# Two more split units a round, as halves through a PSUM bank, in a recommendation tower on one core

## What is computed

```python
for i, (W, b) in enumerate(zip(Ws, bs)):          # three layers, 128 maps each
    z = einsum('bfd,bgd->bfgd', x, h)             # x: (1024, 39, 16), h: 39, then 64 maps
    cur = relu(einsum('bfgd,fgl->bld', z, W) + b)
    if i != 2: h, direct = cur[:, :64], cur[:, 64:]
    else:      direct = cur
    outs.append(direct)
z = concat(outs).sum(-1)                          # over d
h = relu(concat([z, dense_ctx]) @ W_top1 + b_top1)
h = relu(h @ W_top2 + b_top2)
y = h @ W_top3
```

## Time and profile before

| | |
|---|---|
| median of 3 runs | 1290.84 us (1286.87 to 1290.93) |
| the profiled execution's own time | 1292.15 us |
| its span | 1290.1 us |
| granted TensorE clock, mean | 0.996 |
| busy: TensorE, VectorE, ScalarE, GpSimd | 96%, 81%, 58%, 83% |

### The profile page before, as it was taken

One profiled execution on the slowest core, in us unless ns is written; L12 is line 12 of the kernel. 1 busy time (PEld: TensorE's weight loads), 2 busy tenths in 40 slices (PEclk: granted clock), 3 DMA queues, 4 the chain that ended last, 5 costly groups with the idle time before them and its releaser, 6 DMA issues.

```text
span 1290.1 us, 13206 instructions
## 1 busy us (share of the span) xinstructions
PE 1232.2 (96%) x4052; PEld 742.1 (58%) x4052; DVE 1046.8 (81%) x970; ACT 750.6 (58%) x931; POOL 1071.3 (83%) x629
## 2 busy tenths in 40 slices
PE   0598999999999999999999999999999999999999
PEld 0244555665565556655655566556655666666655
DVE  2189888898888888988888888889888888889852
ACT  1136565656655756556556665565566667777743
POOL 7468988888888898888989898888988778888952
PEclk9899999999999999999999999999999999999999
DMA  8194466664444666654446666444456654456100
GB/s 185 24 225 103 110 134 146 146 141 118 110 113 110 138 146 146 141 122 104 116 107 141 145 147 145 113 111 120 112 130 146 145 143 100 117 124 164 50 1 1
DMA packets 102503, 156.09 MB, mean 121 GB/s; under 512 B 20812, under 2 KB 32989, under 8 KB 102323
## 3 DMA queue, kind: packets, MB, share of 16 engines
q1 hardware_dynamic: 92256, 152.56, 49.9%
q0 software_dynamic: 10176, 2.70, 2.2%
HBM read 151.31 MB, written 6.19 MB: 122 GB/s over the span
## 4 chain that ended last, share of the span: by engine, by line
PE 88%; POOL 4%; DVE 3%; issue 3%; ACT 1%; DMA 0%; another core or an unknown queue 0%; DVEq 0%; ACTq 0%; POOLq 0%
PE curM L916 36%; PE curM L939 11%; PE curM L931 11%; PE curM L932 11%; PE curY L916 10%; POOL emb L324 3%; DVE z L596 2%; PE xk L905 2%; PE curY L931 1%; PE curY L932 1%; PE curY L939 1%; POOL zl L335 1%; ACT h L782 1%; DVE zl L658 1%; PE h L1028 0%
## 5 line engine op out<-in xcount | busy, mean ns | idle before, releaser
L335 POOL TENSOR_TENSOR zl<-z,zh 128x1024 fp32r<-128x1024 f32 (+1 forms) x301 | 728.9, 2434 | 116.6 <-ACT zh L748 110.2
L596 DVE TENSOR_TENSOR z<-xr,h 128x1024 f32<-128x1024 f32 x576 | 677.6, 1216 | 137.9 <-PE curM L916 113.7
L748 ACT ACTIVATE zh<-z 128x1024 fp32r<-128x1024 f32 (+1 forms) x376 | 396.2, 1057 | 390.8 <-DVE z L596 229.7
L916 PE MATMUL curM<-z,wf 128*128 128x512 f32 (+2 forms) x1194 | 537.2, 600 | 0.0
L324 POOL DMA_INDIRECT emb<-in_tbl_dram,idx x312 | 335.8, 1076 | 90.1 <-issue 55.4
L931 PE MATMUL curM<-zh,wl 128*128 128x512 f32 (+1 forms) x642 | 339.4, 529 | 2.1 <-issue 1.5
L916 PEld LDWEIGHTS curM<-z,wf 128*128 128x128 f32 (+2 forms) x1194 | 208.2, 188 | 195.0 <-issue 171.2
L932 PE MATMUL curM<-zh,wh 128*128 128x512 f32 (+1 forms) x642 | 251.4, 392 | 0.0
L939 PE MATMUL curM<-zl,wh 128*128 128x512 f32 (+1 forms) x642 | 200.2, 393 | 5.9 <-POOL zl L335 3.6
L931 PEld LDWEIGHTS curM<-zh,wl 128*128 128x128 f32 (+1 forms) x642 | 121.5, 189 | 71.9 <-issue 51.6
L782 ACT ACTIVATE h<-curM,bias 32x512 f32<-32x512 f32 (+1 forms) x198 | 128.0, 646 | 54.3 <-DVE z L596 47.9
(11 more groups left out here) (122 smaller groups left out, 479.0 us busy)
## 6 DMA issues: line engine op xcount, KB each, us to landing
xr<-xT SPq DMA_DIRECT2D x384, 192.0 KB
xs<-xT SPq DMA_DIRECT2D x279, 156.0 KB
xq<-xT SPq DMA_DIRECT2D x64, 256.0 KB
emb<-in_tbl_dram,idx POOLq DMA_INDIRECT x312
xs<-xT SPq DMA_DIRECT2D x62, 78.0 KB
xT<-xc SPq DMA_DIRECT2D x31, 78.0 KB
xr<-in_L_rec_W_dram SPq DMA_DIRECT2D x16, 144.0 KB
xT<-xc SPq DMA_DIRECT2D x31, 40.0 KB
```

Source lines behind the costliest of these rows:

```text
L335: nc.gpsimd.tensor_tensor(zl[0:n, SNUM[r, u] % NL, :], z[0:n, z_slot(r, u), :], zh[0:n, SNUM[r, u] % NH, :], ALU.subtract).then_inc(lo_poo ...
L596: return nc.vector.tensor_tensor(z[:, slot, :].rearrange("p (a n) -> p a n", a=2), x, h, ALU.mult)
L748: nc.scalar.activation(zh[0:n, SNUM[r, u] % NH, :], z[0:n, z_slot(r, u), :], ACT.Copy).then_inc(hi_ready, 1)
L916: mm = nc.tensor.matmul(cur[:, :], wf[rows, full_at(u), a, :], z[rows, z_slot(r, u), a * N:(a + 1) * N], start=start and i == 0, stop=stop ...
```

## The change

It changes five things together:

- `KINDS`: units 1, 6, 12 and 17 become kind **P**, units 4 and 14 go from D to F. A round has nine G, four P and eleven F. P holds in rounds 1 to 30; outside, such a unit is D. The late units of layer 2 are 14 and 19, for 12 and 19.
- A P unit has no buffer in `z`. VectorE multiplies one tile of it (512 columns) into the PSUM bank `curY`, ScalarE copies from there to `zh`, VectorE subtracts from there to `zl`, and then the second tile takes the same bank: first half at the unit's place, first subtraction and second half two units later (`HALF`), second subtraction four units later.
- `curY` is freed by letting the sums of all layers take `curM[0]` and `curM[1]` in turn (`bank`). TensorE may so start a layer only when ScalarE has read the sum before the last: unit 10 waits for all of `take0`, unit 20 for all of `take1`, unit 0 for `take2`. The reads are moved forward on ScalarE.
- `NZ` is 7, over the units that use `z`.
- The weights of the dense inputs (`wC`) share the space of `xs` and are loaded in round 29. The loops over `j` are written out; the program was unrolled before too.

```diff
-KINDS = "GFGFDGFGFF" + "FGFGDFGFGF" + "FGFF"
+KINDS = "GPGFFGPGFF" + "FGPGFFGPGF" + "FGFF"
-NZ, NH, NL = 8, 4, 4
-LAST_AT, SPREAD_AT, COPY_AT = 5, 3, 7
-LATE_A, LATE_C = (3, 8), (12, 19)
+NZ, NH, NL = 7, 4, 4
+IN_PSUM = range(1, STEPS - 1)
+HALF = 2
+LAST_AT, SPREAD_AT, COPY_AT = 1, 3, 7
+LATE_A, LATE_C = (3, 8), (14, 19)
...
-    return 1 if r < 0 else 4
+    return 1 if r < 0 else 2 if r == LAST else 4
...
+        def bank(r, layer):
+
+            if r < 0:
+                return curY if layer == 0 and r != -2 else curM[r == -2]
+            return curM[(r + (layer - 1) % 3) % 2]
...
+                        for u in range(A_END + 3 * k + 1, A_END + 3 * k + 4):
+                            if kind(r, u) == "P" and u + HALF > A_END + 3 * k + 3:
+                                sp.wait_ge(z_second, HALVES[r, u] + 1)
...
+            def product_half(r, u, a):
+
+                done = z_ready if a == 0 else z_second
+                if a == 0 and HALVES[r, u] > 0:
+                    dve.wait_ge(lo_dve, DVE_LO[r, u])
+                if a == 1:
+                    dve.wait_ge(lo_first, HALVES[r, u] + 1)
...
+                nc.vector.tensor_tensor(curY[:, :], xr[s % 2][:, q * N:(q + 1) * N], h[:, a * N:(a + 1) * N],
+                                        ALU.mult).then_inc(done, 1)
+
+            def subtract_half(r, u, a):
+                before = ring_before(r, u, NL)
+                if before is not None:
+                    dve.wait_ge(z_used, NUM[before] + 1)
...
+                nc.vector.tensor_tensor(zl[:, SNUM[r, u] % NL, cols], curY[:, :], zh[:, SNUM[r, u] % NH, cols],
+                                        ALU.subtract).then_inc(lo_dve if a == 1 else lo_first, 1)
...
+                    second, finished = behind(r, u, HALF), behind(r, u, 2 * HALF)
+                    if finished:
+                        subtract_half(*finished, 1)
+                    if second:
+                        subtract_half(*second, 0)
+                        product_half(*second, 1)
+                    if kind(r, u) == "P":
+                        product_half(r, u, 0)
...
+                nc.scalar.activation(zh[:, SNUM[r, u] % NH, a * N:(a + 1) * N], curY[:, :],
+                                     ACT.Copy).then_inc(hi_ready if a == 0 else hi_second, 1)
...
-                    if 11 <= u < 18 and 0 <= r <= STEPS - 3:
-                        take0(r, u - 11, j)
-                    if 0 <= r <= STEPS - 4 and u >= C_END:
-                        for i in range(2 * (u - C_END), min(7, 2 * (u - C_END) + 2)):
-                            take1(r, i, j)
+                    if 0 <= r <= STEPS - 3:
+                        for i in {8: [DIRECT], A_END: [0, 1, 2], A_END + 1: [3, 4], A_END + 2: [5]}.get(u, []):
+                            take0(r, i)
+                    if 0 <= r <= STEPS - 4:
+                        for i in {C_END - 2: [DIRECT], C_END: [0, 1, 2, 3], C_END + 1: [4, 5]}.get(u, []):
+                            take1(r, i)
...
-                        if u == A_END and r >= 1:
-                            pe.wait_ge(read2, r + LOOP * j)
+                        if u == A_END and 1 <= r <= STEPS - 3:
+                            pe.wait_ge(read0, 7 * (r + 3))
```

More of the change, by code:

```diff
@@ L389, in _ @@
             round_(0)
-            for j in range(3):
-                for r in range(1, 1 + LOOP):
-                    round_(r, j)
-            for r in range(LOOPED[1], LAST + 1):
+            for r in range(1, LAST + 1):
                 round_(r)
@@ new lines, in take0, with take1 @@
+                if i == 0 and r >= -1:
+                    act.wait_ge(z_ready, NUM[r, A_END - 1] + 1)
+                take(i, h1, l0_bank(s), bias0, read0, direct[s % 2][0:H, :])
+            def take1(r, i):
+                s = r + 1
+                if i == DIRECT:
+                    act.wait_ge(z_used, NUM[r, A_END - 1] + 1)
+                    if s >= 2:
+                        act.wait_ge(sumA, s - 1)
+                if i == 0:
+                    act.wait_ge(z_ready, NUM[r, C_END - 1 if r >= 0 else UNITS - 1] + 1)
+                take(i, h2, bank(r, 1), bias1, read1, direct[s % 2][H:P, :])
@@ L994, in _ @@
             pick(1)
-            turn(2, 0, 0)
+            turn(2, 0)
             for p in range(2, 4):
```

341 lines of the change are left out of this document (178 added, 163 removed).

## The result

The changed kernel takes 1284.12 us (median of 8 runs, 1283.49 to 1285.18) against 1290.62 us of the kernel before (8 runs). The ratio is 0.9959, 95% interval 0.9945 to 0.9972. The time moved the way that was forecast, but lies 10.5 us above the forecast and outside the 1267 to 1279 that the prediction gave for it; it is inside only of the wider range to 1288 that took in the rival of the gate, which didn't come true in the steady rounds.

A forecast was written before the change was run, and what follows sets the result against it. TensorE was taken to bound the steady rounds: profiled 1292.15 - 18.8 (rounds 1 to 28) - 1.5 (rounds 29 to 31) + 2.3 (start-up) + 0.7 (gates) = 1274.9, as median 1273.6 us. Range 1267 to 1279; to 1288 with the gate.

The forecast's parts named there:

- the rival of the gate: TensorE waits at unit 10 for ScalarE's reads in every round, losing 0.3 us each: 1282 us; chance 0.15.
- the price of an exchange: On TensorE, a split unit in place of a single-precision one saves 0.335 us; two a round, 0.67 us.
- VectorE's load: VectorE would need 34.2 us a round against 36.14 on TensorE, so it holds with 1.9 us to spare.
- The rival in which VectorE becomes the bound: Half operations on VectorE cost more than the 0.64 us taken; at 0.90 us each 1333 us, at 0.82 1299; chance 0.11.
- Start-up: Before the steady rounds, three more VectorE subtractions out of SBUF, two where TensorE waits for VectorE: +2.3 us.
- Two with more split units, -0.1: In rounds 26 to 28, two more split units ahead of unit 10's gate leave a spare time of -0.1 us.
- gave the gates 0.7 us over the run: Allowance of +0.7 us in the sum for TensorE's waits at gates such as unit 10's in rounds 26 to 28.
- Rounds 29 to 31 ... I take 1.5 us: In the last rounds GpSimd sets the pace and is disturbed less: 1.5 us saved, bounds 0 and 3.4.
- the count of the gate at unit 10: TensorE needs seven ScalarE reads before unit 10: spare 0.6 us in rounds to 25, -0.1 in 26 to 28.

The follow-up runs named there:

- tail_best: Changed kernel with round 30's late half subtraction ahead of round 31's sum, layer 1 of round 30 in the transposes' bank, ScalarE's late reads spread: 1274.13 us, ratio 0.9882.
- all_in_sbuf: Changed kernel without the PSUM halves: units 1, 6, 12 and 17 subtracted whole by VectorE out of SBUF in all rounds; 1321.01 us, ratio 1.0261 to the kernel before.
- dve_extra: Changed kernel with one more VectorE product of 512 columns in each of rounds 1 to 24; 1289.34 us, ratio 0.9981 to the kernel before.
- tail_flush: Changed kernel with the second half subtraction of unit 17 of round 30 moved ahead of round 31's sum on VectorE; 1276.09 us, ratio 0.9913 to the kernel before.

## Why the prediction was wrong, step by step

- **What bounds the kernel, and the price of an exchange: right.** 0.62 us a round measured for 0.67; TensorE without a pause from 200 to 1000 us. What makes up the missing 0.05 isn't shown.
- **VectorE's load: right.** (748.21/800) x 36.20 = 33.9 us a round for 34.2. The half operations at 0.69 us show no spread (678 to 695 ns in tail_best), so they escape GpSimd, as the forecast read from the products; all_in_sbuf gives the price of not doing so, 2.06 us. The Trainium skill (SBUF — State Buffer, Who interferes with whom) says the same of instructions with one input in SBUF and with two, and the trace agrees. The rival in which VectorE becomes the bound fell, and dve_extra shows room for 0.68 us more. By the estimate from the Trainium skill (Perfetto Trace Analysis, Optimizing Scalar/DVE Operations), with 1.0 us a round more for PSUM, it would have been 35.2 us. The trace disagrees: of 1024 columns, a product that reads PSUM takes 1206 to 1223 ns, and a subtraction in SBUF alone 1218 at its shortest.
- **Start-up: the size of the term was right, its cause isn't shown, and what surrounds it was missed.** Round 0 lasts 46.5 us instead of 43.9, +2.6 for +2.3. But TensorE's waits in it grew from 4.8 to 6.9 us, and only 0.6 of that is for VectorE's subtractions; 1.1 is for a copy of ScalarE and 0.4 for GpSimd. In the stretch ahead of it, from the transposes of x2, the changed kernel needs 1.9 us less (41.9 for 43.8), which I hadn't looked for and didn't test. And the profiled start of before is one of several lengths. It was luck that the time came well inside the range to 1288: -3.8 us at the start, for which the forecast had no reason, hid a third of what the end lost, and with starts of equal length the gain of some 3 us would have put it at 1287.6.
- **"Two with more split units, -0.1": mis-sized.** I counted rounds 26 to 28 with the steady rounds at 0.67 each, and gave the gates 0.7 us over the run. They took all of it: 107.25 us for 107.10, 2.1 us lost. For unit 10 I had counted 0.1 us too late, and for unit 20 1.3 to spare; TensorE is late by 0.35 us at the one and 0.3 at the other in each of rounds 26 and 27, and the edits show that nothing is won by moving the reads.
- **"Rounds 29 to 31 ... I take 1.5 us": the step that failed.** I asked there only what GpSimd sets, since it set the pace before. I left out my own rule for a moved step, what stands behind and before it in its queue. The half subtraction was moved four units down VectorE's order; in the steady rounds that is free, in round 30 there are no more units between it and the sum of round 31, which waits for ScalarE. And the count of the gate at unit 10 was made for rounds to 28 and not for the rounds in which ScalarE reads all seven at once, where the two banks put `last` behind them. Measured +11.3 us where I had -2.2 (with round 28); tail_best shows 9.8 of it to be just these places, and tail_flush 8.3 of it to be the one subtraction with the clock behind it.
- **The rivals.** None was this one. "The gate binds" was right as a mechanism, in the late rounds alone.

## What to carry to other kernels

When work is moved by a fixed number of units in an engine's queue, write down its place in the last rounds too, where the units it was to hide among run out: a ready instruction of 0.7 us behind one that waits cost 7 us and the clock after it. The steady rounds of this kernel could be forecast to a tenth of a microsecond from one trace; its end needed the same count made separately. And before a few microseconds of the start are put down to a change, take a second profile of the same kernel.

## What the runs showed of the hardware

- A subtraction of VectorE with both inputs in SBUF waits out a whole row of GpSimd's subtractions, 8.37 us once for an operation of 1.2 us, though it had started 0.3 us ahead of the row.
- Behind pauses of TensorE of 2.15 and of 6.9 us most of the next nine to twelve matmuls ran at the spacing of the lower clock, 2.2 and 1.8 us more: the short pause cost double its length. Behind a pause of 1.83 us in tail_best the clock stayed up.
- One input in PSUM costs VectorE nothing that shows: 1.215 us for a product of 1024 columns with one, 1.218 for a subtraction with none. To write the bank as well costs little: 0.692 us for 512 columns where the product of dve_extra, which reads PSUM and writes SBUF, takes 0.679.
- What it costs GpSimd when VectorE subtracts out of SBUF: its gathers take 0.96, 1.07 and 1.27 us with none, two and four such subtractions a round (200 to 1000 us of the changed kernel, the kernel before and all_in_sbuf).
